# Image transformer kernel: the dense sample's rows reach the partitions by transposes instead of through DRAM, and the gather ring holds 35 samples

## What is computed

```
# layer 1: x_proj = x @ w_in + b_in ; offsets and masks from a depthwise 3x3 convolution
def corner(yf, xf, wgt):
    valid = (yf >= 0) & (yf < H) & (xf >= 0) & (xf < W)
    idx = clip(yf) * W + clip(xf)
    return img[idx] * (wgt * valid)
samp = corner(y0, x0, (1-wy1)*(1-wx1)) + corner(y0, x0+1, (1-wy1)*wx1) \
     + corner(y0+1, x0, wy1*(1-wx1)) + corner(y0+1, x0+1, wy1*wx1)
# GROUP = 4 groups of 32 channels, P = 9 points each: 36 samples a token
y = einsum('nghwpc,nhwgp->nhwgc', samp, mask_sm) @ w_out + b_out
x1 = x + gamma1 * layer_norm(y) ; x2 = x1 + gamma2 * layer_norm(gelu(x1 @ w_fc1) @ w_fc2)
# layer 2: softmax attention (Wq, Wk, Wv) on the normalized tokens, residual,
#          then normalized again, router, top 2 of 8 experts, residual
```

## Time and profile before

| | us |
|---|---|
| median of 3 runs | 8871.8 (8868.9 to 8876.0) |
| profiled execution, whole | 8856.8 |
| its span, first to last instruction | 8855.0 |
| GpSimd busy | 6546.0 (74%) |
| PE busy | 5535.4 (63%) |
| VectorE busy | 5200.9 (59%) |
| ScalarE busy | 2368.2 (27%) |

### The profile page before, as it was taken

How to read it: one execution, slowest core, us unless ns; L and a number is a source line. 1 busy time by engine, 2 the same in 40 slices (tenths; PEclk the granted TensorE clock), 3 DMA queues, 4 the chain that set the end, 5 groups by cost and what they waited for, 6 DMA issues and landing times.

```text
span 8855.0 us, 69949 instructions
## 1 busy us (share of the span) xinstructions
PE 5535.4 (63%) x19826; PEld 3066.5 (35%) x19826; DVE 5200.9 (59%) x10762; ACT 2368.2 (27%) x5042; POOL 6546.0 (74%) x6899
## 2 busy tenths in 40 slices
PE   4547575656765577566675567664767566664567
PEld 2224343333432334333333334332433333332334
DVE  4655656556565655666475656655656655655553
ACT  2223222222332233222222222222323222222222
POOL 6777777777777777777777777777777777777771
PEclk7768787777877788777887778876878777776778
DMA  7323333233333323333233323333233323222220
GB/s 104 77 70 70 73 70 78 66 75 70 70 77 69 76 66 73 76 73 71 68 75 72 74 68 72 74 75 69 67 78 71 76 66 65 73 65 65 62 64 15
DMA packets 851804, 624.52 MB, mean 71 GB/s; under 512 B 551035, under 2 KB 734563, under 8 KB 851473
## 3 DMA queue, kind: packets, MB, share of 16 engines
q0 software_dynamic: 221200, 452.53, 21.1%
q1 hardware_dynamic: 629600, 167.72, 11.4%
q10 hardware_dynamic: 672, 0.24, 0.0%
HBM read 549.38 MB, written 70.57 MB: 70 GB/s over the span
## 4 chain that ended last, share of the span: by engine, by line
POOL 57%; issue 21%; PE 12%; DVE 6%; DMA 3%; SPq 1%; ACT 1%; POOLq 0%; DVEq 0%; another core or an unknown queue 0%; ACTq 0%
POOL ring L715 57%; PE bank L1466 2%; PE bank L1500 2%; PE bank L1488 2%; DMA ring<-column_table,idx_r 2%; DVE y L1042 2%; PE bank L1394 1%; PE bank L1651 1%; PE bank L1628 1%; DVE ring L1032 1%; PE bank L1563 1%; SPq L530 1%; DMA tokens<-z 0%; SPq L500 0%; DMA tin<-tokens 0%
## 5 line engine op out<-in xcount | busy, mean ns | idle before, releaser
L715 POOL DMA_INDIRECT ring<-column_table,idx_r x6860 | 6521.9, 951 | 2129.6 <-issue 2069.1
L1032 DVE TENSOR_TENSOR ring<-ring,bank 128x4608 f32<-128x4608 f32 x196 | 970.3, 4950 | 1189.4 <-POOLq L726 1188.2
L1042 DVE TENSOR_REDUCE y<-ring 128x128 f32<-128x4608 f32 x196 | 1572.9, 8025 | 24.3 <-remote 22.3
L1455 PE MATMUL bank<-ident,xh 112*128 112x112 f32 x224 | 56.4, 407 | 1317.0 <-DVE xh L962 1317.0
L1466 PE MATMUL bank<-kT,qT 128*112 128x448 f32 (+3 forms) x1792 | 812.8, 601 | 98.4 <-DVE cmax L1141 62.9
L1152 DVE RECIPROCAL rinv<-bank 112x2 f32<-112x2 f32 x112 | 18.5, 165 | 1307.0 <-PE bank L1513 1307.0
L1500 PE MATMUL bank<-pT,xh 112*128 112x448 f32 (+3 forms) x1792 | 774.2, 514 | 17.6 <-ACT pT L836 15.8
L1488 PE MATMUL bank<-qT,kT 128*112 128x448 f32 (+3 forms) x1792 | 750.4, 504 | 1.2 <-ACT qT L830 1.2
L836 ACT ACTIVATE pT<-bank 112x448 f32<-112x448 f32 (+3 forms) x896 | 451.7, 506 | 820.6 <-PE bank L1488 642.3
L1563 PE MATMUL bank<-xpad,diag 128*128 128x448 f32 x1008 | 492.0, 652 | 235.2 <-ACT xflat L853 184.1
L1141 DVE TENSOR_REDUCE cmax<-bank 112x1 f32<-112x448 f32 (+3 forms) x896 | 506.1, 579 | 187.3 <-PE bank L1466 94.3
(11 more groups left out here) (187 smaller groups left out, 7061.6 us busy)
## 6 DMA issues: line engine op xcount, KB each, us to landing
ring<-column_table,idx_r POOLq DMA_INDIRECT x6860
xflat<-dense_rows SPq DMA_DIRECT2D x56, 406.0 KB
column_table<-proj SPq DMA_DIRECT2D x196, 112.0 KB
corner_weight<-wts_s SPq DMA_DIRECT2D x56, 252.0 KB, 4.5
wts_r<-corner_weight SPq DMA_DIRECT2D x196, 72.0 KB
hT<-dense_rows SPq DMA_DIRECT2D x224, 56.0 KB
tin<-tokens SPq DMA_DIRECT2D x56, 224.0 KB, 3.1
out<-xn SPq DMA_DIRECT2D x56, 224.0 KB
```

The costliest lines, as they stand in the source:

```text
L715: pool.indirect_dma_start(ring[:, r, e * CORNERS:(e + 1) * CORNERS, :].rearrange("p s c -> p (s c)"), None, source, bass.IndirectOffsetOnA ...
L1032: dve.tensor_tensor(corners, corners, wts_p.unsqueeze(2).broadcast_to([128, GP * CORNERS, CG]), ALU.mult)\
L1042: dve.tensor_reduce(y[:, k % BLK % 2].rearrange("p (g c) -> p g c", g=G), ring[:, bass.ds(t % RING, 1)].rearrange("p o (g e) c -> p (o g) ...
```

## The change

The rows no longer go through DRAM, and SP issues none of their transfers. `drow` keeps the six values a token of eight chunks. PE's `spread_rows` transposes a column of it that is read with stride zero, so that all 116 partitions of a PSUM bank get the same row (eight transposes a chunk, ahead of the attention), and `set_places` reads those banks. ScalarE's `widen_weights` repeats the four row weights over 32 columns each into `t1`, PE's `spread_weights` turns them (four transposes), ScalarE copies the result into `part`, and `keep_part` multiplies in place. The ring holds 35 samples, so the multiply covers 140 corner columns instead of 144 and the sum falls into one of three groups and one of the last. DENSE, the number of dense samples, is 1 as before. The output product's second bank is 1 instead of 4 and its first 5. `hats_ahead` is now 5 for every j.

```
-O_BANKS = (4, 5)
+O_BANKS = (5, 1)
...
-FETCHED = GP - 1
+DENSE = 1
+FETCHED = GP - DENSE
...
+STAGES = NB // 2
+ITEMS = DENSE * STAGES
+PLACE_BANKS = ((3, 6), (4, 5))
+SUM_BANKS = (0, 4)
+WEIGHT_BANK = 5
...
-        column_row, stripe_row, place, row_wts = xflat[0:2 * PAD, 0], xflat[0:2 * PAD, 1], hT[0:2 * PAD, 1], hT[:, 0]
...
-        ring = sb("ring", [128, RING, GP * CORNERS, CG])
...
+        drow = sb("drow", [TT, LEAD, DENSE, NT, ROWS_KEPT])
...
+        place = [hT[0:2 * PAD, d] for d in range(DENSE)]
...
+        ring = sb("ring", [128, RING, FETCHED * CORNERS, CG])
...
-            return min(NB // 2 - 1, 2 + j)
+            return max(STAGES, ITEMS + 1 - blocks(j))
...
-            def load_rows(i, j, gd, fronts):
...
-                sp.dma_start(xflat[0:2 * PAD].rearrange("p a n -> p (a n)"),
-                             row_d[gd, 0:2].rearrange("a n -> (a n)").partition_broadcast(2 * PAD)).then_inc(d_rows_in, 16)
-                for dy in range(DY):
-                    sp.dma_start(row_wts[dy * CG:(dy + 1) * CG], row_d[gd, 2 + dy].partition_broadcast(CG))\
-                        .then_inc(d_rows_in, 16)
...
+                for item in range(ITEMS):
+                    hats(dense_chunk(*now)[2], item)
+                widen_weights(dense_chunk(*now)[2], 0)
+                for d in range(DENSE):
+                    keep_weights_spread(*now, d)
+
+            def widen_weights(gd, d):
+
+                act.wait_ge(d_placed, FIRST + gd + 1)
+                act.activation(t1[:, :, :].rearrange("p t (r c) -> p t r c", r=DY),
+                               drow[:, gd % LEAD, d, :, 2:].unsqueeze(3).broadcast_to([TT, NT, DY, CG]), ACT.Copy)                    .then_inc(d_weights_wide, 1)
+
+            def keep_weights_spread(p, f, d):
+
+                gd = dense_chunk(p, f)[2]
+                if gd >= 2:
+                    act.wait_ge(z_made, FIRST + p * PAIR_TILES + (f - 2) // 2 * BLK + (BLK if f % 2 else PARTS[0][1]))
+                act.wait_ge(d_weights_spread, FIRST + gd * DENSE + d + 1)
+                act.activation(part[:, f % 2, d], bank[WEIGHT_BANK][:, 0:CH], ACT.Copy).then_inc(d_weights_kept, 1)
+                if d + 1 < DENSE:
+                    widen_weights(gd, d + 1)
...
                 if now:
-                    for stage in range(ahead):
-                        hats(gd, stage)
+                    act.wait_ge(experts_read, FIRST + g)
+                    widen_weights(gd, 0)
+                    for item in range(ahead):
+                        hats(gd, item)
...
+                    if now and b < DENSE:
+                        keep_weights_spread(*now, b)
                     if b == 0 and second:
                         project_first(*second)
-                    if now and 1 <= b <= NB // 2 - ahead:
+                    if now and 1 <= b <= ITEMS - ahead:
                         hats(gd, ahead + b - 1)
...
-                dve.tensor_reduce(
-                    y[:, k % BLK % 2].rearrange("p (g c) -> p g c", g=G),
-                    ring[:, bass.ds(t % RING, 1)].rearrange("p o (g e) c -> p (o g) c e", g=G), AX.X, ALU.add)\
-                    .then_inc(y_made, 1)
+                terms = ring[:, bass.ds(t % RING, 1)].rearrange("p o e c -> p (o e) c")
+                whole = (G - 1) * P9 * CORNERS
+                step.did(dve.tensor_reduce(
+                    y[:, k % BLK % 2, 0:(G - 1) * CG].rearrange("p (g c) -> p g c", c=CG),
+                    terms[:, 0:whole].rearrange("p (g e) c -> p g c e", g=G - 1), AX.X, ALU.add))
+                step.wait()
+                dve.tensor_reduce(y[:, k % BLK % 2, (G - 1) * CG:], terms[:, whole:].rearrange("p e c -> p c e"),
+                                  AX.X, ALU.add).then_inc(y_made, 1)
...
             def set_places(gd):
 
-                dve.wait_ge(d_rows_in, (gd + 1) * (16 * (1 + DY)))
-                step.did(dve.tensor_scalar(column_row, column_row, dcol[0:2 * PAD, NB + 1:NB + 2], 1.0, ALU.subtract, ALU.min))
-                step.wait()
-                dve.scalar_tensor_tensor(place, column_row, -1.0, stripe_row, ALU.max, ALU.add).then_inc(d_placed, 1)
+                dve.wait_ge(d_rows_spread, FIRST + gd + 1)
+                for d in range(DENSE):
+                    step.did(dve.tensor_scalar(place[d], bank[PLACE_BANKS[d][0]][0:2 * PAD, 0:CH],
+                                               dcol[0:2 * PAD, NB + 1:NB + 2], 1.0, ALU.subtract, ALU.min))
+                for d in range(DENSE):
+                    step.wait()
+                    ins = dve.scalar_tensor_tensor(place[d], place[d], -1.0, bank[PLACE_BANKS[d][1]][0:2 * PAD, 0:CH],
+                                                   ALU.max, ALU.add)
+                    if d < DENSE - 1:
+                        step.did(ins)
+                ins.then_inc(d_placed, 1)
...
-                dve.tensor_tensor(part[:, f % 2], bank[0][:, 0:CH], row_wts, ALU.mult).then_inc(d_kept, 1)
+                dve.wait_ge(d_summed, FIRST + (gd + 1) * (NB * DENSE))
+                dve.wait_ge(d_weights_kept, FIRST + gd * DENSE + DENSE)
+                for d in range(DENSE):
+                    step.wait()
+                    ins = dve.tensor_tensor(part[:, f % 2, d], bank[SUM_BANKS[d]][:, 0:CH], part[:, f % 2, d], ALU.mult)
...
                     sum_up(*second)
+                if now:
+                    keep_part(*now)
...
-                    if now:
-                        keep_part(*now)
...
+            def spread_rows(gd):
+
+                pe.wait_ge(f_iw_made, FIRST + gd + 1)
+                rows = drow[:, gd % LEAD]
+                for d in range(DENSE):
+                    for r in range(2):
+                        for t in range(NT):
+                            ins = pe.transpose(bank[PLACE_BANKS[d][r]][0:2 * PAD, t * TT:(t + 1) * TT],
+                                               rows[:, d, t, r:r + 1].broadcast_to([TT, 2 * PAD]), ident[0:TT, 0:TT])
+                ins.then_inc(d_rows_spread, 1)
+
+            def spread_weights(gd, d):
+
+                pe.wait_ge(d_weights_kept, FIRST + gd * DENSE + d)
+                pe.wait_ge(d_weights_wide, FIRST + gd * DENSE + d + 1)
+                for t in range(NT):
+                    ins = pe.transpose(bank[WEIGHT_BANK][:, t * TT:(t + 1) * TT], t1[:, t, :], ident[0:TT, 0:TT])
+                ins.then_inc(d_weights_spread, 1)
+
+            def sum_columns(i, gd, item):
+
+                d, stage = item // STAGES, item % STAGES
+                if item == 0:
                     pe.wait_ge(d_stripes_in, (i + 1) * 64)
-                pe.wait_ge(d_hat_made, FIRST + gd * (NB // 2) + stage + 1)
+                pe.wait_ge(d_hat_made, FIRST + gd * ITEMS + item + 1)
...
+                banks_left((0, LEAD), 0, 0)
+                spread_rows(gd)
+                for item in range(ITEMS):
+                    sum_columns(i, gd, item)
+                for d in range(DENSE):
+                    spread_weights(gd, d)
...
                 banks_left(fronts, s * 2 + h, g)
+                if now:
+                    spread_rows(gd)
...
+                if now:
+                    pe.wait_ge(d_placed, FIRST + gd + 1)
...
-                if now:
-                    sum_columns(di, gd, 0)
+                    if now:
+                        sum_columns(di, gd, q)
                 pe.wait_ge(max_made, FIRST + g + 1)
...
-                    for stage in range(1, ahead):
-                        sum_columns(di, gd, stage)
+                    spread_weights(gd, 0)
+                    for item in range(NT, ahead):
+                        sum_columns(di, gd, item)
...
-                    if now and 1 <= b < NB // 2 - ahead:
+                    if now and 1 <= b <= ITEMS - ahead:
                         sum_columns(di, gd, ahead + b - 1)
-                if now:
-                    sum_columns(di, gd, NB // 2 - 1)
```

126 lines of the change are left out of this document (55 added, 71 removed).

## The result

The changed kernel takes 8839.5 us (median of seven executions, 8836.3 to 8844.5) against 8868.9 us (8860.6 to 8876.0) for the kernel before in the same comparison: ratio 0.9968, 95% interval 0.9956 to 0.9979. That is 29 us less; 8.5 had been forecast. In another comparison the ratio was 0.9971 (0.9960 to 0.9981). Every trace shows one execution only. That of the kernel before took 8856.8 us, less than any of its seven timed ones, so between the two traces the gain is 19.5 us and not 29.

A forecast was written before the change was run, and what follows sets the result against it. GpSimd's stream of 6860 gathers, 1.257 us each, was taken to bound the kernel. Gains of 4 us (contention), 2 (transfers) and 2.5 (tail) summed to 8.5, from 8871.8 to 8863 us; range 8846 to 8884.

The forecast's parts named there:

- Step 1: Rows' DRAM store and loads go: nobody on the path waits for them; at most 11 us of landing waits, 2 taken.
- more than thought: Rival: small packets and SP's issues, not VectorE, cause the long gathers; 8810 us, half of it 8840; chance 0.10.
- Step 2: VectorE's two place operations read PSUM, not two SBUF rows, so gathers lengthen less: gain 4 us, bounds 0 and 7.
- Steps 3 to 5: PE's row transposes (2 us), ScalarE's spreading (0.6) and copy (0.54) hidden, cost 0; VectorE's place operations 0.1 us slower.
- Step 4: VectorE's place operations with one PSUM source: 0 to 0.15 us more each, 0.1 taken, on the path at j=3 alone.
- Steps 6 to 8: Tail, dense units: sums behind each score group, turned weights +1.8 us; fifth hats leave the loop -0.8; last sum leaves -2.0.
- steps 7 and 8: Exponentials' loop in the tail: fifth stage of hats leaves it, gain 0.8 us; last sum leaves its end, gain 2.0.
- step 7: Fifth stage of hats leaves the exponentials' loop: gain 0.8 us at j=4, nothing at j=3.
- Step 9: VectorE's product of sum and weights moves from behind the second normalization to the exponentials' loop: gain 0.6 us a unit, 1.2.
- Step 10: Ring of 140 corner columns for 144: multiply 0.14 us shorter, sum stays at 8.0; 0.4 us gained in the tail.

The follow-up runs named there:

- e2: Kernel before with the row store and the five row loads left out (dense sample wrong): 8847.5 us, ratio 0.9986.
- e17: Kernel before without its row transfers, the edit of e2, on a later chip: 8848.7 us, ratio 0.9983.
- e4: Kernel before with the row store left out and the five loads kept, read from x: 8850.2 us, ratio 0.9988.
- e1: Kernel before, unchanged, run again for a second trace: 8861.4 us, ratio 1.0001.
- e3: Kernel before with the five row loads left out and the 4-byte store kept: 8861.1 us, ratio 1.0000.
- e5: Changed kernel, unchanged, run again on another chip for a second trace: 8854.5 us, ratio 0.9971 to the kernel before.
- e6: Changed kernel with the store in 4-byte pieces put back, nobody reading it: 8889.3 us, ratio 1.0009 to the kernel before.
- e7: Changed kernel with the ring of 36 samples, multiply over 144 columns and sum in one instruction: 8859.1 us, ratio 0.9975 to the kernel before.
- e18: Changed kernel with dense sums behind the fourth score group and GpSimd's wait and report behind the fourth gather: 8841.2 us, ratio 0.9976 to the kernel before.
- e12: Changed kernel with dense sums behind the fourth score group, on a chip where GpSimd did not bound: ratio 0.9763 to the kernel before.
- e8: Changed kernel with four more two-SBUF-input VectorE instructions a chunk, 224 in all: 8869.1 us, ratio 0.9986 to the kernel before.
- e11: Kernel before with GpSimd's wait and report of a tile behind the twelfth gather, not the sixth, where GpSimd did not bound: ratio 0.9997.
- e15: Kernel before with GpSimd's wait and report behind the twelfth gather, as e11, on a second chip where GpSimd did not bound: ratio 1.0003.

## Why the prediction was wrong

**Step 1 (row transfers, taken as 2 of at most 11 us) failed, and it carries most of the miss.** The edit is worth 13.4 us (e2) and 14.4 (e17), most of it from the store. I had seen the landings' 11 us in the earlier trace rows and put most of them down to the start and "one place". The six gaps that exceed 0.305 us by more than 0.3 come to 11.0 us there, each at a tile whose last landing was late, and each ends 12 to 21 us behind a store's issue. Only three of the six lie in the first 400 us. Two things misled me: that nobody waits for the rows themselves, which is no cost to VectorE but says nothing of the queue beside it, and that the engines are busy for a third of the time, where they were 98% busy for the 13 us that counted. The bound of 11 was also not quite one, since the gaps without a store lie 2 us below 6859 times 0.305, and it was read from an execution faster than all the timed ones.

**The rival "more than thought" named the small packets rightly and their effect wrongly.** It had the small packets lengthen the gathers; they delay the landings. Without the store the durations' excess is 48.3 (e2), 49.1 (e4) and 51.6 (e17), with it 46.1, 43.8 and 51.6 (before, e1, e3). That the measured time lies in this rival's range (8810 to 8854) is therefore luck.

**Step 2 (contention, 4 us) held in mechanism and roughly in size.** The six traces with the old L1104 and L1106 average 48.4 us of duration excess, the five with the new places (the changed kernel, e5, e6, e7, e18) 44.1: 4.3 us. Single traces scatter by 8 us, so the 5 us that the first pair of traces showed were no measurement by themselves. Plainer is the count behind step 2, made again: of 68 gathers beside L1106 21 exceeded 1.0 us; beside its successor L1118, which reads one SBUF row and a PSUM bank, none of 63 does, and beside the product none of 75. Beside L1114, L1104's successor, it is 14 of 87 with 1.3 us of excess, against 16 of 84 with 3.3. The excess beside the two of the places, partly of the same gathers, goes from 7.0 us (12.3 in e1) to 1.4 (1.4 in e5).

**Steps 3 to 5 held, with small misses.** The eight L1413 of j = 4 took 0.95 us and PE then idled 14.51 us. Copy and widening took 0.54 and 0.62. Step 4 was under its size: the PSUM-reading L1114 takes 676 ns where L1104 took 445, 0.23 more and outside the bound of 0.15.

**Steps 6 to 8 failed together: forecast -1.0 us (1.8 for the weights, -0.8, -2.0), measured +0.9 at the clock of before and up to +4.1 at a lower one.** PE's timeline at j = 4 of the changed kernel, to be held against the earlier trace rows:

```profile
8446.04 4.84 PE L1516 MATMUL bank<-kT,qT 128*112 128x448 f32 x10 [0.63 <-ACT qT L823]
...
8468.39 0.93 PE L1526 MATMUL bank<-ident,nmax 112*1 112x112 f32 x8
8469.25 0.61 PE L1422 MATMUL bank<-ident,t 112*128 112x112 f32 x4
8469.69 1.88 PE L1433 MATMUL bank<-arena,stripes 116*128 116x448 f32 x4
8471.50 1.76 PE L1539 MATMUL bank<-qT,kT 128*112 128x448 f32 x4
...
8502.70 1.13 PE L1564 MATMUL bank<-wv,xnT 128*112 128x129 f32 x8 [0.63 <-ACT xnT L847]
8510.14 0.98 PE L1657 MATMUL bank<-ident,xn 112*128 112x112 f32 x4 [6.31 <-issue]
```

From the first block product (L1539) to the output product it is 31.2 us; in the trace of before L1488 starts at +157.55 and L1513 at +190.77 from the multiply, 33.2 us. Those 2.0 us are steps 7 and 8 as forecast. But from the first scores to the first block product it is 25.5 us, against 23.5 before. A stage of the sums had left the loop and now stood ahead of it: on PE, which is the path here, it took 1.5 to 1.9 us there. I had booked what left and not what arrived. "The same ten matmuls remain" was right and was the very reason why taking one from the end gives nothing on an engine that never idles. At j = 4 the two cancel: 56.7 us from scores to output product against 56.8. At j = 3 there was no wait of step 7 to win, and it is 50.3 against 47.7. There the first sum ran at a lower granted clock, as its length shows beside the next one, and beside the first sum of e6:

```profile
8329.28 3.10 PE L1433 MATMUL bank<-xflat,stripes 116*128 116x448 f32 x4
...
8335.32 1.68 PE L1433 MATMUL bank<-arena,stripes 116*128 116x448 f32 x4
```
```profile
8358.17 1.68 PE L1447 MATMUL bank<-xflat,stripes 116*128 116x448 f32 x4
```

In e6, the same code for PE, it is 48.6 us at j = 3 and 56.7 at j = 4: 0.9 us more than before in all, at a mean granted clock from first scores to first block of 0.90 and 0.94 (before: 0.91 and 0.93). That is what the stage ahead of the blocks and the turned weights cost; what lies above it goes with the clock: 2.6 and 2.5 us in the two traces of the changed kernel (0.88 and 0.94; 0.90 and 0.89), 4.1 in e7 and e18 (0.82 and 0.89). These last two are also the test of the interleaving, which e18 takes out: 50.2 and 58.2 us in both, with 4.6 us less to the row of maxima in e18 and as much more behind it. So the interleaving costs nothing, and my theory in e12 and e18, that it delays the maxima to no use, fell. Another 0.9 us of the 2.2 lies between the turning of xn at j = 3 and the first product of j = 4 (61.5 against 60.6 us); no run takes it apart.

**Step 9 held:** from the output product to the turning of xn it is 7.44 us instead of 7.89 at j = 4, and 7.14 instead of 7.87 at j = 3. **Step 10** held: the multiply went from 4.96 to 4.82 us. The stretch from tile 192 to the end is 303.4 to 303.6 us in six traces with the old order, and 302.2 to 302.4 in e5, e7, e8 and e18, 1.2 less. In the changed kernel's first trace it is 299.9 (300.0 in e6), because PE's last feed-forward products ran at a higher granted clock: 0.84 from 8705.4 to 8714.3, against 0.50 from 8721.4 to 8734.2 before. Its last part shows it, before and after:

```profile
8728.69 5.49 PE L1439 MATMUL bank<-w_fc,arena 128*128 128x128 f32 x24 [0.67 <-ACT arena L786]
```
```profile
8711.33 2.95 PE L1485 MATMUL bank<-w_fc,arena 128*128 128x128 f32 x24 [0.67 <-ACT arena L767]
```

The two levels of this clock are 1.2 and 2.4 GHz; 0.50 is the lower one. These 2.4 us come and go between executions of the changed code (two of six traces have them, none of the six of the old code), so one trace can't count them as a gain; whether the change makes them more frequent is not shown.

**Not foreseen: the start.** The first gather begins at 50.8 to 52.1 us in six traces with the change and at 52.1 to 53.0 in six without, 1.3 us on the average. e7 rules the ring's size out; the cause is open.

**The sum, and what stays open.** Store 12, contention 4, start 1, tail nothing or a microsecond lost: 16 to 17 us, and by the measured pair 14.4 + 7.5 = 22 on the last chip. On the two chips of the result and of e5 the change brought 29 and 27. The kernel before was slower there (8868.9 and 8881.8 against 8863.1 and 8860.9), the changed kernel with the store put back lost 35, and both point to a store that costs more on some chips. Against it: on e5's chip the kernels without a store, e5 and e7, also took 7 to 18 us more in the executions that have no trace than in the one that has. The kernel without transfers was not run on those two chips, so the last 5 to 7 us are not shown to be the store's, and their cause is open. That the six-gather wait alone turns late landings into loss is read from four traces (before, e1, e3, e6); the kernel meant to undo it (e11, e15) never ran where GpSimd bounds.

## What to carry to other kernels

A transfer that nobody waits for is free only if it doesn't share its 13 us with one that somebody waits for: look at how busy the DMA engines are beside each odd wait, not on the average, and count thousands of 4-byte pieces as a delay of some 10 us for whatever else is about to land. When work on the path's own engine is moved, book both ends, what leaves one place and what arrives at the other; on an engine that never idles only what vanishes is gained. And where a gain is the sum of waits of 2 to 4 us that depend on how two loops meet, one profiled execution bounds it poorly: sum all the gaps over the usual one and ask what stands next to each.

## What the runs showed of the hardware

- In the 13 us behind one store of 10.5 KB in 2688 pieces of 4 bytes the 16 DMA engines were 97 to 98% busy (e3, e1) instead of 40% (e2). Where it met the end of a tile, the other queue's last landing came 7.4 to 12.5 us behind the last gather instead of 1.5. SP's next issue took 2.1 to 2.3 us instead of 0.34.
- A VectorE instruction with two SBUF inputs (116x448, 0.62 us) lengthened the gathers by 0.04 to 0.09 us on the average (e8); beside one of the same form with one input in PSUM none of 63 gathers exceeded 1.0 us.
- GpSimd's report of a tile takes effect with the landing, 1.5 us behind the tile's last gather, although it stands behind the fourth (e18) or the sixth gather of the next tile. That the records of the gathers run behind what the engine has already issued would explain it.
- On two of the chips PE stood still for up to 74 us at a time at places where the profile names nothing, at a mean granted clock of 0.66 to 0.68 instead of 0.77 to 0.78, and the kernels took 14000 us instead of 8860. Many of the standstills have one length: ahead of L1454 more than half of those over 10 us last 23.4 to 24.3 us, on both chips. The packets that load instructions (queue q8) are as many as in e5 and no longer (1.10 us against 1.12), so slower loading of code is not what the traces show. What stops PE there was not found.
